# Folded bias columns as rows in four column tiles, and later steps for two output products, at the seam of a decoder layer's last two phases

## The reference

```
eq  = x @ me_eq_w + me_eq_b
sym = (eq @ me_wv + me_bv) @ me_wo + me_bo
e1  = gelu(sym @ me_c1w + me_c1b) @ me_c2w + me_c2b
...
h2  = layer_norm(syn + attn) * ce_n1g + ce_n1b
ff  = relu(h2 @ ce_f1w + ce_f1b) @ ce_f2w + ce_f2b
...
e0  = (silu(x @ sw_w1) * (x @ sw_w3)) @ sw_w2
```

## Time and profile before

| what | value |
|---|---|
| median of 3 runs | 1589.13 us (1588.66 to 1591.57) |
| profiled execution | 1590.26 us, of which the span of instructions 1588.5 us |
| TensorE busy | 1521.3 us, 96% of the span |
| VectorE busy | 1141.3 us, 72% |
| ScalarE busy | 847.6 us, 53% |
| granted TensorE clock, mean | 0.972 |

### The profile page before, as it was taken

One profiled execution on the slowest core, in us unless ns is written; L12 is line 12 of the kernel. 1 busy time (PEld: TensorE's weight loads), 2 busy tenths in 40 slices (PEclk: granted clock), 3 DMA queues, 4 the chain that ended last, 5 costly groups with the idle time before them and its releaser, 6 DMA issues.

```text
span 1588.5 us, 28790 instructions
## 1 busy us (share of the span) xinstructions
PE 1521.3 (96%) x11272; PEld 1079.8 (68%) x11272; DVE 1141.3 (72%) x2311; ACT 847.6 (53%) x1121; POOL 367.9 (23%) x399
## 2 busy tenths in 40 slices
PE   6999999888799999999999899999999999999998
PEld 3333333334466666666657788898989888888887
DVE  5445556456789999999964788767676777777675
ACT  4888889764588888888873242222222122222221
POOL 0000001221546665666461320000000000000000
PEclk8999999986799999999998999999999999999999
DMA  7765665444467575665652100000000000000000
GB/s 146 136 109 119 127 119 97 83 76 88 62 97 112 77 110 92 103 97 79 97 172 67 32 29 14 1 1 14 1 14 1 14 1 14 1 1 14 1 14 14
DMA packets 61575, 97.24 MB, mean 61 GB/s; under 512 B 12588, under 2 KB 29880, under 8 KB 61440
## 3 DMA queue, kind: packets, MB, share of 16 engines
q1 hardware_dynamic: 60928, 94.62, 32.1%
q10 hardware_dynamic: 512, 0.79, 0.3%
HBM read 26.16 MB, written 4.19 MB: 19 GB/s over the span
## 4 chain that ended last, share of the span: by engine, by line
PE 88%; DVE 7%; ACT 3%; issue 1%; DMA 1%; POOL 0%; POOLq 0%; SPq 0%; ACTq 0%; DVEq 0%
PE ps L109 83%; PE ps L1134 2%; ACT PX L1301 1%; ACT H L538 1%; DVE NM L1356 1%; DVE EE L660 1%; PE ps L1096 1%; PE ps L1142 1%; DVE XC L1961 1%; PE ps L1066 1%; PE ps L1769 0%; DMA QT<-XSb 0%; PE ps L1760 0%; DVE XH L573 0%; DVE X L585 0%
## 5 line engine op out<-in xcount | busy, mean ns | idle before, releaser
L1356 DVE TENSOR_REDUCE NM<-ps 128x4 f32<-128x1024 f32 x256 | 307.9, 1220 | 49.1 <-PE ps L109 47.8
L1301 ACT ACTIVATE PX<-ps 128x1024 f32<-128x1024 f32 x256 | 262.4, 1025 | 82.2 <-PE ps L109 81.0
L538 ACT ACTIVATE H<-ps,b1c 128x1024 f32<-128x1024 f32 x256 | 268.5, 1118 | 38.7 <-PE ps L109 37.1
L1921 ACT ACTIVATE GF<-ps,cols 128x512 f32<-128x512 f32 x128 | 88.2, 689 | 295.7 <-PE ps L109 295.7
L109 PE MATMUL ps<-XC,W_sw_w 128*128 128x512 f32 x768 | 187.3, 395 | 0.0
L109 PEld LDWEIGHTS ps<-XC,W_sw_w 128*128 128x128 f32 x768 | 141.6, 190 | 28.3
L2112 DVE CAST GH<-GF 128x512 fp32r<-128x512 f32 x192 | 82.1, 427 | 106.9 <-ACT GF L1921 101.7
L2220 POOL TENSOR_SCALAR RSc<-AGc 128x4 f32<-128x4 f32 x23 | 6.9, 302 | 602.4 <-DVE AGc L2007 602.4
L109 PE MATMUL ps<-PX,VT 128*32 128x256 f32 x2048 | 140.9, 394 | 1.6 <-DVE X L585 1.5
L1916 ACT ACTIVATE GF<-ps 128x512 f32<-128x512 f32 x64 | 38.2, 597 | 188.5 <-PE ps L109 188.5
L109 PE MATMUL ps<-KT,QT 48*128 48x512 f32 x512 | 133.6, 522 | 5.1 <-DMA QT<-XSb 3.1
(11 more groups left out here) (233 smaller groups left out, 2569.3 us busy)
## 6 DMA issues: line engine op xcount, KB each, us to landing
ST<-QS SPq DMA_DIRECT2D x256, 96.0 KB, 2.8
KT<-KS SPq DMA_DIRECT2D x128, 192.0 KB, 4.7
QT<-XSb SPq DMA_DIRECT2D x120, 96.0 KB, 4.2
XT<-in_xT_dram SPq DMA_DIRECT2D x8, 512.0 KB, 4.3
raw_a<-in_x_dram SPq DMA_DIRECT2D x8, 512.0 KB, 4.4
CR<-in_ctxT_dram SPq DMA_DIRECT2D x8, 512.0 KB, 4.8
out_dram<-X SPq DMA_DIRECT2D x7, 512.0 KB, 3.3
R_sw_w<-in_sw_w_dram SPq DMA_DIRECT2D x6, 512.0 KB, 5.3
```

Source lines behind the costliest of these rows:

```text
L538: e.activation(H1[s % 8][:, :, :], PP[s % 3][:, :, :], ACT.Tanh, bias=b1c[:, half:half + 1], scale=1.0).then_inc(act_th, 1)
L1301: e.activation(PX[s % 3][:, :, :, :], PP[2][:, :, :].rearrange("p g (c q) -> p g c q", c=2), ACT.Exp, bias=0.0, scale=0.25).then_inc(act_e ...
L1356: e.tensor_reduce(NM[u % 2][:, qc, :, :, i], PP[qc][:, :, :].rearrange("p g (m k) -> p g m k", m=2), AX.X, ALU.max, negate=True).then_inc( ...
L1921: e.activation(g[:, :], o, f, bias=cols[:, col:col + 1], scale=1.0).then_inc(act_g, 1)
```

## The change

Two things change.

Fold 12 becomes two folds. The bias vectors now come from the host repeated over 32 columns (`rows4`). The new fold 12 multiplies each of the four vectors, as a weight of 32 columns, by its matrix of 512 moving columns: 8 matmuls, which write four groups of 32 partitions (column tiles) of bank 4. VectorE copies that bank to `BS`, 128 x 512. Fold 13, after step NS + 2, turns rows into columns: four matmuls whose weights are 128 x 128 pieces of `BS` and whose moving operand `sums` has two columns, one that selects and adds the first three row groups and one that selects the fourth. VectorE adds the eight numbers to `cols`. Those who waited for 13 folds now wait for 14.

Of the last token group's four outputs, the first moves from step 265 to 267 and the third from 273 to 275. They thus stand one chunk later on TensorE, and their additions to X one chunk later on VectorE.

```
-    FB = Place(M, 0)("FB", [128, 8976])
+    FB = Place(M, 0)("FB", [128, 9228])
...
-                p = due(s, 41 + 8 * b + 4 * qc, 32, NP)
+                p = due(s, 41 + 8 * b + 4 * qc, 32, NP - 1)
                 if p is not None:
                     return p, b, qc
+                if s == (NS + 11, NS + 13, NS + 19, NS + 21)[2 * b + qc]:
+                    return NP - 1, b, qc
...
     def fold_due(s):
-        return due(s, NS - 12, 1, 13)
+        return 13 if s == NS + 2 else due(s, NS - 12, 1, 13)
...
-            b = f % 2 if f < 12 else 4
-            if f == 12:
+            b = f % 2 if f < 12 else f - 8
+            if f >= 12:
                 w.wait_ge(act_ex, NS)
...
+            elif f == 12:
+                for k in range(2):
+                    for v, m in enumerate((R2, R1, T["me_c1w"], T["ce_f1w"])):
+                        t = mm(e, P[b][32 * v:32 * v + 32, :], rows4[:, v, k, :], m[:, k, :], k == 0, k == 1)
             else:
-                for col in range(8):
-                    at = 128 * (col % 4)
-                    for v, m in ((0, R2), (1, R1), (2, T["me_c1w"])) if col < 4 else ((3, T["ce_f1w"]),):
-                        for k in range(2):
-                            t = mm(e, P[b][:, col:col + 1], m[:, k, at:at + 128], vb[:, v, k:k + 1], col == 0 and v == 0 and k == 0, True)
+                w.wait_ge(dve_fold, 13)
+                for c in range(4):
+                    t = mm(e, P[b][:, 2 * c:2 * c + 2], BS[:, 128 * c:128 * c + 128], sums, c == 0, True)
             t.then_inc(pe_fold, 1)
...
+                elif f == 12:
+                    t = e.tensor_copy(BS, o)
                 else:
-                    t = e.tensor_tensor(cols[:, 0:8], cols[:, 0:8], o[:, 0:8], ALU.add)
+                    c8 = cols[:, 0:8].rearrange("p (x c) -> p c x", x=2)
+                    t = e.tensor_tensor(c8, c8, o[:, 0:8].rearrange("p (c x) -> p c x", x=2), ALU.add)
...
-                w.wait_ge(b_end["folds"], 13)
+                w.wait_ge(b_end["folds"], 14)
```

More of the change, by code:

```diff
@@ L842, in phase_b @@
     vc = FB[:, n + 512:n + 1024].rearrange("p (v k n) -> p v k n", v=2, k=2)
-    vb = FB[:, n + 1024:n + 1032].rearrange("p (v k) -> p v k", v=4)
-    v2 = FB[:, n + 1032:n + 1288].rearrange("p (k n) -> p k n", k=2)
+    v2 = FB[:, n + 1024:n + 1280].rearrange("p (k n) -> p k n", k=2)
+    vb = FB[:, n + 1280:n + 1538]
+    rows4 = vb[:, 0:256].rearrange("p (v k m) -> p v k m", v=4, k=2)
+    sums, BS = vb[:, 256:258], T["me_eqT"].rearrange("p k n -> p (k n)")
     PRODUCTS = ((RI, T["ce_wvT"], T["ce_wo"], 256, 0), (R1, T["me_woT"], T["me_c1w"], 512, 0), (Wce, T["ce_synT"], RI, 256, 2),
@@ L1401, in step @@
             if f is not None:
-                o = P[f % 2 if f < 12 else 4]
+                o = P[f % 2 if f < 12 else f - 8]
                 w.wait_ge(pe_fold, f + 1)
@@ L2392, in col @@
         return Fn[name].reshape(-1, 128).T
-    r["vb"] = np.stack([col(k) for k in ("me_eq_b", "me_bv", "me_bo", "ce_n1b")], 1)
+    vb = np.stack([col(k) for k in ("me_eq_b", "me_bv", "me_bo", "ce_n1b")], 1)
+    sums = np.stack([(p % 32 == 0) & (p < 96), p == 96], 1).astype(f)
+    r["vb"] = np.concatenate([np.repeat(vb.reshape(128, 8), 32, 1), sums], 1)
     r["vc"] = np.stack([np.repeat(col(k)[:, :, None], 128, 2) for k in ("ce_syn_b", "ce_bv")], 1)
```

## The result

The changed kernel took 1583.08 us in the median of 7 runs (1581.18 to 1586.83), the kernel before 1589.94 us (7 runs, 1587.22 to 1591.57). The ratio is 0.9962 with a 95% interval of 0.9949 to 0.9974, so the change makes the kernel faster by 0.38%, some 6 us. Forecast were 5.4 us. Two more sets of rounds of the same kernel gave 0.9961 (0.9947 to 0.9976) and 0.9958 (0.9944 to 0.9973).

A forecast was written before the change was run, and what follows sets the result against it. TensorE, 96% busy, was taken as the bound, with VectorE's queue counting at the seam. Gains of 7.7 + 1.1 = 8.8 us less 3.4 for low clock gave 5.4 us: 1583.7 us, range 1580.0 to 1587.5.

The forecast's parts named there:

- the first part: Fold 12 to chunk 0, with the new folds: chunk 0 starts at 862.8 against 870.51, 7.7 us gained.
- the low stretches: TensorE's clock at 1.2 instead of 2.4 GHz: two or three stretches of some 3.4 us, costing 3.4 us together.
- the wait for `PR`: TensorE idle ahead of the matmuls on `W_ce`: 1.9 to 2.0 us, where it waited 0.90.
- The wait that takes the place: Second and fourth last outputs wait for additions to X instead of `OH`: 2.75 and 2.5 us.
- The clock afterwards: After the three new TensorE waits, two or three short stretches at the low clock, 1.4 us each on average: 3.4 us lost.
- The second part as a whole: Chunk 0 to chunk 7, with the moved outputs: chunk 7 starts at 906.2 against 907.28, 1.1 us gained at full clock.
- A clock that stays up: Rival: after the new waits the clock stays up, or falls once: 1580.3 to 1581.9 us, 20%.
- The column tiles did overlap: Rival claimed the opposite: fold 12 still takes some 7 to 9 us, 1586 to 1589 us in all, 4%.
- the second rival: Longer stretches at the low clock after the waits, such as 10.2 us: 1586.4 us, with two 1589.7, 16%.

The follow-up runs named there:

- The kernel with 64 columns: Kernel before, with 64 equal moving columns instead of one in each of old fold 12's 32 matmuls: 1585.04 us, ratio 0.9971.
- The kernel with bank 7: Changed kernel, with the second and fourth of the last outputs in bank 7 instead of bank 6: 1575.96 us, ratio 0.9927 against the kernel before.
- the pairs: Changed kernel with outputs two and four in bank 7, ScalarE copying fold 12's rows, and the first two outputs directly behind each other: 1576.17 us, ratio 0.9912.

## Why the prediction was right

The time and the sum held: 5.4 us forecast, 5.17 in the seam and about 6 by the ratio. That the sum came so close is in part luck, since its errors cancel: the first part brought 0.3 us more than forecast (7.96, not 7.7), the second 0.8 less (0.3, not 1.1: 36.77 before against 37.99 less one low stretch of 1.56), and the low stretches cost 0.3 less (3.1, not 3.4). Point by point:

- **Up to chunk 0.** Forecast were 7.7 us, measured 15.93 - 7.97 = 7.96. Fold 12 took 1.83 to the next row (1.85 forecast, from `H,w2p`), the wait for `PR` 1.71 (1.9 to 2.0), `W_ce` 2.96 (3.0), fold 13 0.81 (0.85). The wait came out shorter in part because the copy held `ZR` up by 0.57 us (855.44 to 856.01 in VectorE's timeline) and not 0.7. In one of the two other profiles of the changed kernel a low stretch after this wait made the 7.97 us 9.48. The kernel with 64 columns bears out that a good half of the gain is clock and not work: 4.3 to 4.9 us of it, where the prediction had 3.7 (7.7 less some 4).
- **The wait that takes the place.** The prediction had the wait for `OH` turn into one for the first addition, through the shared half bank, and the same for the third and fourth output. The kernel with bank 7 shows this cause: the waits went when the bank was another. The second of them was sized right (2.5, measured 2.49), the first was not: 2.75 forecast, 3.53 measured. The term that was mis-sized is VectorE's piece from chunk 2's product to the addition: 3.61 + 4.96 = 8.57 forecast, 881.51 - 872.30 = 9.21 measured. All of that is in two small instructions of the routing, 0.60 and 0.41 us, which took 0.17 each before. They take 0.60 and 0.41 us in every profile with the moved outputs, and 0.16 or 0.17 in every one without. There the first of them runs beside GpSimd's product `ON`, which takes 1.02 us instead of 0.62; before, it ran beside another instruction of GpSimd's and was not slower. No run separates the two engines, so the cause is open.
- **The clock afterwards.** Two or three low stretches of some 3.4 us were forecast, and in the three profiles of the changed kernel there are two each. The first wait, for `PR`, was followed by one in one of the three. In the profile shown, the stretch in chunk 7 cost 4.51 - 2.94 = 1.57 us and the one in the second output and chunk 5 about as much, (1.58 - 0.98) + (3.90 - 2.94) = 1.56. The price was right, and the number at the lower end of what was said.
- **The second part as a whole.** Its sum reads "1.1 us gained", at a full clock. That is against a seam that contains a low stretch of 1.56 us, so at an even clock it is already a loss of 0.5 us. With the two and a half new low stretches taken off it is a larger one, as the sum has it: 5.4 - 7.7 = -2.3 us; measured, 5.17 - 7.96 = -2.8. The prediction didn't ask what the folds alone would give. The runs answer that: the moved outputs alone make the kernel slower by 0.27%, and beside the new folds they cost 1.6 to 2.7 us in the seam, 1.1 to 1.2 of it in the queues at an even clock. So the first part brings the gain and the second takes some of it back. The prediction's numbers imply that, but its text doesn't say it.
- **The rivals.** A clock that stays up did not occur with the changed kernel, and did with bank 7, whose waits are of 1.71 and 2.53 us. The column tiles did overlap: the new fold's 16 records of 512 columns took 1.90 us, as long as 4 such records over the full width did in an earlier fold (1.88 us). Fold 13's two columns per matmul, which the second rival names, did no harm: in none of the nine profiles that have it was its 0.8 us followed by a low stretch. Low stretches longer than 3.4 us appeared at the seam only with the old fold, and in one profile of the folds alone (872.04 to 876.90 for one chunk there, 4.9 us instead of 2.8, and 0.7 more in the output ahead of it).

## What to carry to other kernels

A wait that is moved out of the way comes back through the resource that its owner holds: before moving a step in one engine's queue, look in which order the other engine will release the bank, and give the second user another bank if there is one; that was worth 7.4 us in the seam here (5.6 by the ratios), more than the change brought in the seam. Take the two parts of a change apart before forecasting their sum: here one brought the gain and the other cost some of it. Where an engine is saturated over a stretch, as VectorE is from chunk 2 to chunk 5, a wait removed on TensorE can turn up behind the next instruction that needs that engine, as 1.98 us of 2.53 did with the pairs. The fold of one-column matmuls cost more than its own time here, since what followed it ran at the lower clock. Turning the product round, so that the matrix moves, removed that, and so did giving it 64 columns.

## What the runs showed of the hardware

- 64 records of one column took 9.13 and 11.38 us in two profiles, 64 with 64 columns 7.36 us. The wider matmuls were faster here, by the clock: it stayed at the upper level in their profile and fell in the two others. A run of 32 records of one column was followed by a low stretch too, the 8 records of two columns in fold 13 were not. The Trainium skill, "TensorEngine Tiling (Array Packing)", section on performance considerations, instruction overhead, has a matmul of one column take as long as one of 60. At the upper level the runs come near that, 0.10 us per record with one column against 7.20 / 64 = 0.11 with 64, each with its own weight load.
- Whether a wait of TensorE's is followed by a low stretch is not settled by its length in this range. Counted at the seam over the 13 profiles, of 10 waits of 3.04 to 3.55 us 8 were followed by one (or had it begin in them), of 7 waits of 2.49 to 2.53 us 3, of 12 waits of 1.71 to 1.98 us 3, and of 3 waits of 1.1 us none. The same kernel has it in one profile and not in the next: its wait of 3.5 us was followed by one in two profiles of three. One such stretch costs about 1.5 us, a quarter of what the whole change brought.
